# Attention, time-mix, first routing and first experts in one block of instructions, with the tokens of each expert listed by indirect stores

## What is computed

```python
x = x + cross_attention(layernorm(x), ctx)            # ctx: 257 rows a sequence, and the own 32
xn = layernorm(layernorm(x)) * g1 + b1                # time-mix
xx = shift(xn)
k, v, r = (xn*mu + xx*(1-mu)) @ (Wk, Wv, Wr)          # each with its own mu, r through a sigmoid
# recurrence over the 32 tokens of a sequence, for each channel:
#   wkv_t = (e1*aa + e2*v_t) / (e1*bb + e2);  aa, bb, pp are updated with decay w
x2 = layernorm(x) + (r * wkv) @ Wo
ei = layernorm(x2) * g2 + b2
top2, weights = softmax(ei @ router_w), two of eight experts
exx = shift(ei)
for e: out_e = sigmoid(xr_e @ eWr[e]) * (square(relu(xk_e @ eWk[e])) @ eWv[e])
x = x + x2 + sum of the two chosen out_e, weighted
x = x + shared_geglu(layernorm(x)) + geglu of the best of 8 experts
```

## Time and profile before

| | us |
|---|---|
| median of 3 runs (1023.16 to 1024.01) | 1023.5 |
| the profiled execution | 1025.3 |
| its span, first to last instruction | 1023.6 |
| attention | 0 to 156.5 |
| time-mix | 157.5 to 304.3 |
| first routing | 312.4 to 340.4 |
| first experts | 340.6 to 541.9 |
| the rest | 544 to 1023.6 |

### The profile page before, as it was taken

The page is one execution under the profiler, slowest core; times in us unless marked ns, Lnnn a source line. Parts: engine busy times, 40 slices in busy tenths (PEclk is TensorE's granted clock), DMA queues, the critical chain, the costliest instruction groups (busy, mean ns, idle before and its releaser), DMA issues. The chain is left out here.

```text
span 1023.6 us, 19906 instructions
## 1 busy us (share of the span) xinstructions
PE 893.4 (87%) x6694; PEld 809.5 (79%) x6695; DVE 438.7 (43%) x1126; ACT 291.2 (28%) x648; POOL 279.8 (27%) x520
## 2 busy tenths in 40 slices
PE   6899987889850499999995999995899999999995
PEld 4566657888840399999994999995799999999994
DVE  2354445999956455555552333335211111111113
ACT  1333324666620254554441111110011111111110
POOL 1664442444443232232203222220210010010006
PEclk8999998999965599999997999997999999999998
DMA  9887828511110242222212111010588988899715
GB/s 348 290 291 276 303 83 285 147 42 32 33 39 4 93 161 86 80 79 87 77 51 63 32 42 37 31 31 27 196 315 331 321 300 327 305 317 326 276 58 164
DMA packets 97918, 163.40 MB, mean 160 GB/s; under 512 B 10136, under 2 KB 76184, under 8 KB 95672
## 3 DMA queue, kind: packets, MB, share of 16 engines
q1 hardware_dynamic: 85552, 120.84, 34.4%
q0 software_dynamic: 6528, 19.54, 7.0%
q10 hardware_dynamic: 5776, 22.22, 5.4%
HBM read 146.06 MB, written 16.52 MB: 159 GB/s over the span
## 5 line engine op out<-in xcount | busy, mean ns | idle before, releaser
L1306 PEld LDWEIGHTS bank<-zT_f,we 128*128 128x128 f32 x1472 | 167.8, 192 | 3.3 <-issue 1.5
L1306 PE MATMUL bank<-zT_f,we 128*128 128x128 f32 x1472 | 168.3, 275 | 1.6 <-issue 1.1
L1323 DVE TENSOR_TENSOR hT_f<-bank,act_g 128x512 f32<-128x512 f32 x78 | 53.8, 691 | 230.4 <-PE bank L1306 217.1
L1315 ACT ACTIVATE act_g<-bank 128x512 f32<-128x512 f32 x78 | 46.6, 597 | 323.7 <-PE bank L1306 323.7
L1306 PE MATMUL bank<-zT_c,a_x 128*128 128x128 f32 x1024 | 122.7, 283 | 0.3 <-PEq L978 0.3
L1306 PEld LDWEIGHTS bank<-zT_c,a_x 128*128 128x128 f32 x1024 | 120.5, 199 | 0.8 <-issue 0.7
L726 PE MATMUL bank<-xn,mixed_w 128*128 128x128 f32 x768 | 94.0, 280 | 1.3 <-ACT xn L808 0.9
L726 PEld LDWEIGHTS bank<-xn,mixed_w 128*128 128x128 f32 x768 | 90.0, 195 | 2.3 <-ACT xn L808 1.3
L1330 PE MATMUL bank<-we,hT_f 128*128 128x256 f32 x368 | 83.3, 380 | 0.0
L1183 PE MATMUL bank<-xk,wk_e 128*128 128x128 f32 x624 | 78.0, 280 | 0.2
L1183 PEld LDWEIGHTS bank<-xk,wk_e 128*128 128x128 f32 x624 | 74.5, 196 | 0.9 <-DVE xr L1237 0.5
(11 more groups left out here) (227 smaller groups left out, 1286.7 us busy)
## 6 DMA issues: line engine op xcount, KB each, us to landing
we<-in_W_dram SPq DMA_DIRECT2D x69, 1024.0 KB, 7.3
ctx_sb<-in_ctx_n_dram ACTq DMA_DIRECT2D x16, 1152.0 KB, 7.4
kT<-in_ctx_t_dram SPq DMA_DIRECT2D x16, 1028.0 KB, 8.9
rows_y<-y SPq DMA_DIRECT2D x39, 128.0 KB, 1.7
ewk_sb<-in_eWk_dram SPq DMA_DIRECT2D x1, 4096.0 KB, 14.2
ewv_sb<-in_eWv_dram SPq DMA_DIRECT2D x1, 4096.0 KB
rows_f<-yr ACTq DMA_DIRECT2D x23, 128.0 KB, 6.2
ewr_sb<-in_eWr_dram SPq DMA_DIRECT2D x1, 2048.0 KB, 19.8
```

Of the source, the lines that this page charges most:

```text
L1306: last = nc.tensor.matmul(bank[half][:, f * P:(f + 1) * P], w12[:, i, k, col0:col0 + P], zT[:, k], start=k == 0, stop=k == KD - 1)
L1315: nc.scalar.activation(act_g[:, half], bU[half][:], ACT.Gelu).then_inc(self.ac_g, 1)
L1323: nc.vector.tensor_tensor(hT[:, parity, half * HH:(half + 1) * HH].rearrange("p f t -> p (f t)"), bG[half][:], act_g[:, half], ALU.mult).t ...
```

## The change

Stages 1 to 4 become one block. There is no barrier between them; what a barrier kept apart is now kept apart by semaphores. All tiles lie in two hand-carved areas, so that the expert weights, which lie over attention's tiles, are loaded after the last residual of attention (`dv_x1`, G).

- Time-mix step j is issued on each engine behind attention step 15 + j (`MIX_AT` = G - 1), so attention steps 16 and 17 stand between time-mix steps 0, 1 and 2. Time-mix has steps 0 to 21.
- On DVE the scan `bb` now writes to a PSUM bank, so `denominator` reads one operand from SBUF and one from PSUM. The decay is put into the other operand of the running maximum, and `key_rise` is one instruction in place of two. The product num * 1/den (`quotient`) stays on DVE.
- ACT copies the logits out, which hold the bias by a one-row product on PE.
- Routing is spread over the steps: for chunk s-5, DVE takes the largest eight, their places, the one-hot rows, their sum, the rank (from two bf16 products on PE) and the slot `expert * 2048 + rank`: seven small instructions. POOL adds the counts up (`count`), and for chunk s-6 stores the token numbers by two indirect DMAs at these slots in a DRAM list `tab_e` (`list_tokens`). Behind the last step DVE computes which expert and which 128 places of the list each tile has (`tile_map`).
- The two gate weights are a sigmoid of the difference of logits, computed in the experts' stage.
- In the experts' stage the 128 token numbers of a tile come from `tab_e` by a DMA that SP issues (`load_pick`), three tiles ahead, at the head of its body of a tile; POOL waits for it, copies the mixing factors and gathers.
- The sixteen small loads of `cm_mu` are part of one larger load.

```diff
-    nc.clear_and_free_semaphores(att_sems)
-    nc.all_engine_barrier()
...
-routing("r1_", 2, NT1, logits, True, table1, expert1, slot1, gate, add_x2)
...
-                nc.gpsimd.tensor_copy(pick[:, s.slot], table1[:, bass.ds(s.n, 1)]).then_inc(picked, 1)
-                wait_picked(pool, 0, s)
-                nc.gpsimd.indirect_dma_start(out=pair[:, s.slot], out_offset=None, in_=rows_e[0:TOK, :],
-                                             in_offset=bass.IndirectOffsetOnAxis(ap=pick[:, s.slot], axis=0)
-                                             ).then_inc(got[s.slot], 16)
...
+def mix_sync(sp):
+    sp.wait_ge(po_mix, 1)
+    sp.dma_start(rows_e.rearrange("(b s) d -> b s d", s=S)[:, 0, 0:D], zero_rows[:]).then_inc(zero_out, 16)
+    sp.dma_start(tab_e.rearrange("(p f) o -> p (f o)", p=P), zero_tab[:]).then_inc(zero_tab_out, 16)
+    sp.wait_ge(dv_x1, G)
+    sp.dma_start(ewk_sb.rearrange("p e (k f) -> p e k f", k=KD),
+                 eWk.rearrange("e (k p) f -> p e k f", p=P)).then_inc(ld_moe[0], 16)
+    sp.dma_start(ewr_sb.rearrange("p e (k f) -> p e k f", k=KD),
+                 eWr.rearrange("e (k p) f -> p e k f", p=P)).then_inc(ld_moe[1], 16)
+    sp.dma_start(ewv_sb.rearrange("p e (k f) -> p e k f", k=FKC),
+                 eWv.rearrange("e (k p) f -> p e k f", p=P)).then_inc(ld_moe[2], 16)
+    sp.dma_start(r2_w[:], Wg.rearrange("(k p) e -> p k e", p=P)).then_inc(ld_s, 16)
+    for n in range(G):
+        sp.wait_ge(po_ei, n + 1)
...
+    def list_tokens(n):
+        if n == 0:
+            pool.wait_ge(zero_tab_out, 16)
+        pool.wait_ge(dv_slot, n + 1)
+        for k in range(2):
+            nc.gpsimd.indirect_dma_start(out=tab_e[:, :],
+                                         out_offset=bass.IndirectOffsetOnAxis(ap=listed[:, n, k:k + 1], axis=0),
+                                         in_=token[:, n:n + 1], in_offset=None).then_inc(po_tab, 16)
...
+    def ranks(n):
+        pe.wait_ge(dv_mask, n + 1)
+        need(pe, po_sum, n)
+        need(pe, dv_prod, n)
+        pe.wait_ge(dv_x2, min(n + 2, G))
+        nc.tensor.matmul(bX[:, D:D + E], before_m[:], mask[:, n % 2], start=True, stop=False)
+        nc.tensor.matmul(bX[:, D:D + E], ones_m[:], earlier[:, n % 2], start=False, stop=True).then_inc(pe_rank, 1)
+    def totals():
+        pe.wait_ge(po_sum, G)
+        pe.wait_ge(dv_prod, G)
+        nc.tensor.matmul(bX[:, 0:E], ones_m[:], earlier[:, G % 2], start=True, stop=True).then_inc(pe_tot, 1)
...
+    def weight_sum(n):
+        nc.vector.tensor_tensor_scan(bB[:, 1:D], e1b[:, n % 2, 0:D - 1], e2b[:, n % 2, 0:D - 1], 0.0, ALU.mult, ALU.add)
+    def denominator(n):
+        nc.vector.tensor_tensor(den[:, n % 2], e_in[:, n % 2], bB[:, 0:D], ALU.add)
...
+    def tile_map():
+        dve.wait_ge(pe_tot, 1)
+        nc.vector.tensor_tensor(cmp_eg, bX[:, 0:E].unsqueeze(2).to_broadcast([P, E, G]),
+                                tile_lo[:].unsqueeze(1).to_broadcast([P, E, G]), ALU.is_gt)
+        nc.vector.reduce_sum(n_tiles[:], cmp_eg, AX)
+        nc.vector.tensor_tensor_scan(t_end[:], ones_e[:], n_tiles[:], 0.0, ALU.mult, ALU.add)
+        nc.vector.tensor_tensor(cmp_te, t_end[:].unsqueeze(1).to_broadcast([P, NT1, E]),
+                                iota_t[:].unsqueeze(2).to_broadcast([P, NT1, E]), ALU.is_le)
+        nc.vector.reduce_sum(te_f[:], cmp_te, AX)
+        nc.vector.tensor_scalar(expert1[:], te_f[:], float(E - 1), None, ALU.min)
+        nc.vector.tensor_tensor(cmp_te, cmp_te, n_tiles[:].unsqueeze(1).to_broadcast([P, NT1, E]), ALU.mult)
+        nc.vector.scalar_tensor_tensor(te_f[:], te_f[:], float(CAP_T), iota_t[:], ALU.mult, ALU.add)
+        nc.vector.reduce_sum(tb_f[:], cmp_te, AX)
+        nc.vector.tensor_tensor(place1[:], te_f[:], tb_f[:], ALU.subtract).then_inc(dv_map, 1)
+    def step(s):
+        b, w, x, h = live(s - 1), live(s - 2), live(s - 3), live(s - 5)
+        if s == 0:
+            dve.wait_ge(po_mix, 5)
...
+    def step(s):
+        b, w, x, h = live(s - 1), live(s - 2), live(s - 3), live(s - 5)
+        if s == 0:
+            dve.wait_ge(po_mix, 5)
+            dve.wait_ge(po_set, 1)
+        if s == 2:
+            nc.vector.memset(bB[:, 0:1], 0.0)
+        if w is not None:
+            decayed(w)
+        if h is not None:
+            largest(h)
+        dve.drain()
+        if w is not None:
+            weight_sum(w)
+        if h is not None:
+            largest_at(h)
+        if w is not None:
+            value_sum(w)
+        dve.drain()
+        if h is not None:
+            one_hot(h)
+        if w is not None:
+            new_value(w)
+            denominator(w)
+        dve.drain()
+        if h is not None:
+            both(h)
+        if b is not None:
+            running_max(b)
+            dve.drain()
+            key_rise(b)
+        if w is not None:
+            gated(w)
+            dve.drain()
+            inverse(w)
+        if x is not None:
+            residual(x)
+        if h is not None:
+            own_rank(h)
+        dve.drain()
+        if w is not None:
+            quotient(w)
+        if x is not None:
+            stats(x)
+        if h is not None:
+            sum_rank(h)
+        dve.drain()
+        if x is not None:
+            moments(x)
+        if h is not None:
+            slots(h)
+        if s == MIX_STEPS - 1:
+            tile_map()
+    return step
...
+def moe_sync(sp):
+    def load_pick(s):
+        at = sp.value_load(place1[0:1, bass.ds(s.n, 1)], min_val=0, max_val=T_ROWS // P - 1)
+        sp.dma_start(pick[:, s.slot], tab_e[bass.ds(at * P, P), :]).then_inc(m_pick[s.slot], 16)
+    sp.wait_ge(dv_map, 1)
+    sp.wait_ge(po_tab, 2 * G * 16)
+    for i in range(NM):
+        load_pick(Step(0, i, NM))
+    def body(s):
+        ahead = s.back(-NM, NT1)
+        if ahead:
+            sp.wait_ge(m_pa, s.n + 1)
+            load_pick(ahead)
+        if isinstance(s.n, int) and s.n in (18, 19):
+            sp.wait_ge(m_x12, G)
+            i = s.n - 18
+            sp.dma_start(ws12[:, i], (w1s, w2s)[i].rearrange("(k p) h -> p k h", p=P)).then_inc(ld_s, 16)
+        if isinstance(s.n, int) and s.n == 20:
+            sp.dma_start(ws3, w3s.rearrange("(f p) d -> p f d", p=P)).then_inc(ld_s, 16)
+        sp.wait_ge(m_dy, s.n + 1)
+        sp.dma_start(rows_y[bass.ds(s.n * P, P), :], y[:, s.slot]).then_inc(m_put[s.slot], 16)
+    sweep(sp, NT1, 21, NM, body, NM)
+    for i in range(NM):
+        sp.wait_ge(m_put[i], NT1 // NM * 16)
...
+    pool.wait_ge(zero_out, 16)
+    for i in range(2):
+        pool.wait_ge(ei_out[i], OUT_PER * G // 2)
+    pool.wait_ge(dv_map, 1)
+    def body(s):
+        e = pool.value_load(expert1[0:1, bass.ds(s.n, 1)], min_val=0, max_val=E - 1)
+        need(pool, m_dx, s.n - NM + 1)
+        pool.wait_ge(m_pick[s.slot], s.lap * 16 + 16)
+        nc.gpsimd.tensor_copy(mu_e[:, s.slot], cm_mu[:, :, e]).then_inc(m_mu, 1)
+        nc.gpsimd.indirect_dma_start(out=pair[:, s.slot], out_offset=None, in_=rows_e[:, :],
+                                     in_offset=bass.IndirectOffsetOnAxis(ap=pick[:, s.slot], axis=0)
+                                     ).then_inc(m_got[s.slot], 16)
+        if isinstance(s.n, int) and 2 <= s.n < 2 + G:
+            c = s.n - 2
+            nc.gpsimd.tensor_tensor(x1[:, c], x1[:, c], a_x2[:, c], ALU.add).then_inc(m_x12, 1)
+    sweep(pool, NT1, 18, NM, body, 0)
+    routing_constants()
...
+        att, mix = att_tensor(pe), mix_tensor(pe)
+        for s in range(ATT_STEPS):
+            att(s)
+            if s >= MIX_AT:
+                mix(s - MIX_AT)
+        for s in range(ATT_STEPS - MIX_AT, MIX_STEPS):
+            mix(s)
```

More of the change, by code:

```diff
@@ new lines, in perceiver_block @@
+        logits = sb("logits", [P, G, E])
+        top = sb("top", [P, G, 8])
+        top_at = sb("top_at", [P, 2, 8], U32)
+        hot = sb("hot", [P, G, 2, E])
+        listed = sb("listed", [P, G, 2], U32)
+        moved = sb("moved", [P, E])
+        moved_k = sb("moved_k", [P, G, 2])
+        mask = sb("mask", [P, 2, E], BF16)
+        earlier = sb("earlier", [P, 2, E], BF16)
+        hot_rank = sb("hot_rank", [P, 2, E])
+        rank = sb("rank", [P, 2])
+        token = sb("token", [P, G], I32)
@@ new lines, in perceiver_block @@
+        N3 = 3
+        in_a = Carve(arena_a, FLOATS_A)
+        w_T = in_a.take(4, KD, D)
+        early = in_a.take(EARLY)
+        bq_c, bk_c = early[:, 0:KD], early[:, KD:2 * KD]
+        bv_b, bo_b = early[:, 4:4 + D], early[:, 4 + D:4 + 2 * D]
+        ctx_sb = in_a.take(N3, BG * TC * D + D)
+        kT = [in_a.take(BG, KD, KW) for _ in range(N3)]
+        hn, v_own, o_nat = (in_a.take(2, D) for _ in range(3))
+        hnT, qT, oT = (in_a.take(2, KD, P) for _ in range(3))
+        prob = in_a.take(2, KW)
@@ new lines, in perceiver_block @@
+        probT = in_a.take(2, 3, P)
+        lora_sb = Carve(arena_b, FLOATS_B).take(8, D)[0:R]
+        in_b = Carve(arena_b, FLOATS_B)
+        z_in = in_b.take(2, D)
```

(48 more changed lines are left out.)

1660 lines of the change are left out of this document (821 added, 839 removed).

## The result

The changed kernel takes 1183.2 us (median of 4 runs, 1171.5 to 1187.9) where the kernel before takes 1023.75 (1023.2 to 1025.5): 1.154 times as long, 95% interval 1.145 to 1.162. The forecast was 1053 us and at most 1080. The direction was right, the size far off: +159 us in place of +29.6.

A forecast was written before the change was run, and what follows sets the result against it. Bounds: DVE in time-mix, serial DVE work in routing, PE in the experts. Terms -4.9 + 3.4 - 26.6 + 56.7 + 1 (block end) = +29.6 on 1023.6 gave 1053 us, range 1031 to 1080.

The forecast's parts named there:

- The seam: Between attention and time-mix: first recurrence 2.4 us early and cheaper steps without routing, together 4.9 us gained.
- The time-mix step: Twelve full time-mix steps: each grows from 8.12 to about 8.4 us, +3.4 us in all.
- The loop over two steps: Time-mix dependency from moments through PE, ACT's logits and DVE's routing to later moments: 16.7 us, 8.35 to 8.4 a step.
- The tail: From the last full time-mix step to the experts' first transposes: 60.6 us shrinks to 33.9, -26.6 us.
- The experts: Experts' stage: list read waits behind a store of y; 18 tile pairs take 12.8 us each, +56.7 us.
- rival 2: Experts' stage: gaps bring PE's half clock, 1.7 us lost at each of 18, adding 31 us: 1084 us; chance 0.12.
- Rival 1: Experts' stage: the read ahead is in time, PE never stands still, only gains remain: 996 us; chance 0.09.
- Rival 3: Time-mix: POOL bounds if an indirect store costs 2 us, not 1.25; +10 us, 1063 us; chance 0.11.

The follow-up runs named there:

- own waits: Changed kernel with the three drains of POOL's time-mix step replaced by waits for a semaphore the instruction itself raises: 1132.9 us, 1.1045 of the kernel before.

## Why the prediction was wrong, step by step

Two terms failed. The two indirect stores a step were priced by their issue alone, and their landing, for which POOL's next drain waits, was put at nothing: 81.2 of the 126.9 us that the profile is over the forecast (52.8 + 28.4). And the slower clock behind each gap was kept as a rival and given no term in the sum: most of the 44.5 us of the experts.

**The seam (-4.9).** The interlocked waits that I walked out are real, but I still gave 2.4 us to the overlap; measured are 0.8 us against before and 0.0 against the kernel without overlap. The other 2.5 us don't follow from my own figures: three steps at 7.0 to 7.4 in place of 7.7 give 0.9 to 2.1. Measured without stores, the three steps behind the first recurrence take 21.9 us, where before they take 23.0: 1.2 us.

**The time-mix step (+3.4).** The loop over two steps was right: 8.42 us measured, 8.35 to 8.4 forecast, in nine of the twelve full steps of the kernel without stores; the first step with routing takes 9.83. The whole stage without stores is 124.1 us against my 121.3. (My sum of DVE's work alone was off: 8.12 less 0.92 plus 0.9 is 8.1, not 7.9. Nothing hung on it, since the loop is longer.) The term that failed is "two indirect stores a step ... 1.25 each": the issue was priced, correctly, and the landing was not priced at all. I wrote that POOL's 6.2 us fit under 8.4, and did not ask what the next drain on POOL waits for. A drain looked free, since before it takes 1.2 us behind ordinary instructions. This stage came out 52.8 us over the forecast, and 50.0 of them go when the stores go (174.1 to 124.1).

**The tail (-26.6).** The same drain stands in the last four steps, where POOL waits 5.0 to 6.8 us each time, and SP waits for the last landing: 62.3 us in place of 33.9. With no stores this stretch takes 322.6 - 290.1 = 32.5 us, with 64-byte rows and own waits 325.6 - 291.8 = 33.8. The walk of this part was right to within 1.5 us; only the stores were missing.

**The experts (+56.7).** The step where I chose against the change was right in kind, and in the number of pairs: PE waits for the gather 18 times behind the first tiles, 3.7 us in the mean. The page's row has all of it, 85.3 us with the 17.9 before the very first transposes:

```profile
L1172 PE MATMUL bank<-ident,arena_b 128*128 128x128 f32 x156 | 32.2, 343 | 86.4 <-DMA arena_b<-rows_e,pick 85.3
```

But a pair takes 15.2 us in the mean, not 12.8. Mean of the 18 pairs, link by link: from the transposes to SP's store of y 7.28 (forecast 5.47); store to read 1.25 (1.3); read to copy 2.23 and copy to gather 0.66 (2.7 together); gather to transposes 3.81 (3.3). The first link is the clock: rival 2 came on top of the forecast, it was no alternative. Behind the gap of 3.75 us in the pair shown above the granted clock is at 0.74 for 6 us, between the levels of 1.2 and 2.4 GHz:

```profile
482.00:488.00 6.00, 5.85 (x30) 5.62 (x31) 2.47 (x6) 2.42 (x4) 1.91 (x3) 0.74 0.15 44
488.00:497.00 9.00, 5.44 (x36) 4.67 (x34) 3.10 (x8) 2.35 (x4) 1.90 (x3) 1.00 0.23 58
```

The transposes take 1.11 in place of 0.60 and the hidden products 2.97 in place of 1.95, 1.5 us in this pair. Other pairs lose more or nothing: in four of the 18 the first link takes 5.5 to 5.6 us, as at full clock, and the pair 13.2 to 13.6; in the other 14 it takes 6.9 to 8.7, and the pair 14.8 to 16.6. Since this chain goes through y, the slower clock lengthens the chain and not only PE's work. The sum of the miss, 44.5 us: the first link 18 x 1.81 = 32.6, nearly all of it the clock, the gather 18 x 0.51 = 9.2, the rest 2.7. Rival 2 had 1.7 us a gap, 31 in all.

The Trainium skill (TensorE: Matmul & The Clock Gate, HAM oscillation), which I had beside rival 2, describes a kernel that a DMA wait at every tile throws back to the slow clock each time. The traces agree in the main, with 0.86 over the stage and 1.00 once the gaps are gone; but behind three of the gaps (3.56 to 3.81 us) the transposes ran at once at full pace, 0.65 us. The fixed cost of 2.0 us, which I had from the Trainium skill (DMA: Bandwidth & Descriptors, Anatomy of one DMA), stands there for DMAs of the GpSimd path, while the read of a list is SP's; it landed in 2.0 us too (median of 39).

**The rivals.** Rival 1 (read in time, 996 us) did not happen; with the order mended, own waits and wide rows the chip comes to 1000 us. Rival 2 (0.12) was true beside the forecast. Rival 3 (0.11) named the right place, POOL in time-mix, and the wrong price: an issue of 2 us, not a wait for landing of 8. The range was wrong in two ways: the cases were treated as excluding each other, and the unknown operation, a store that no trace of before shows, was bounded by a gather's issue on both sides. The gather's landing, 3.3 us, was in the earlier trace rows, and would have been the nearest row to bound it with from above, though a store of 4-byte rows took twice that (6.4).

**What stays open.** Why a store of 4-byte rows lands so late: whether the length of the writes or the distance of the rows counts, and whether rows wider than 64 bytes land sooner still, was not tried. For two stores of 4 bytes the trace gives no time to landing; that the drain ends with it is read from the kernels with one store and with 64-byte rows, where it ends 0.1 us behind the second store's landing.

## What to carry over

Before you put an indirect DMA on POOL, look for drains behind it on POOL: each lasted here until the landing, and a wait for a semaphore that the instruction raises for itself doesn't. A store of single words landed late here and one of 64-byte rows didn't, so pad the rows. And where a queue issues both a result's store and a later tile's read, put the read where nothing of the pipeline's end stands ahead of it: here a change of order by two tiles, with no byte moved otherwise, was worth 100 us.

## What the hardware showed unexpectedly

- A POOL drain behind an indirect store ends 0.1 us after the store's landing. Its record, which covers the work still ahead of it, is 1.3 us with no indirect store, 6.8 with one of 128 x 4 bytes, 9.5 with two, 16.5 with two to neighbouring rows and 5.3 with two of 128 x 64 bytes (medians). The instruction between store and drain runs at once.
- Small indirect stores hold up others: beside them SP needed up to 14.24 us to issue its four stores of 31 KB, 1.5 in a quiet step; with 64-byte rows POOL never waited for them. The Trainium skill (DMA: Bandwidth & Descriptors, Specifications) says that below 512 bytes a transfer is a read, a modification and a write. The runs agree that stores of 4-byte rows are slow; most of the gain is there at 64 bytes already, with first transposes at 325.6 where they come at 345.8 to 350.8 with 4-byte rows and at 322.6 without stores.
- Idle time of PE doesn't hide its slower clock when the chain that makes the gaps runs through PE: pairs whose products ran slowly behind the gap took 14.8 to 16.6 us, the four at full pace 13.2 to 13.6, although PE had about 3.7 us of idle time in each.
